# Graph attention edges: four runs per partition with sums of their own, and a stitch of 512 runs

## The reference

```python
feat = (h @ W).reshape(n, H, F)                    # H = 4 heads of F = 64
e = leaky_relu(el[src] + er[dst], 0.2)             # el, er: a score per node and head
m = segment_max(e, dst); ex = exp(e - m[dst])
a = ex / segment_sum(ex, dst)[dst]
out = segment_sum(feat[src] * a[:, :, None], dst)  # then + b, elu
```

## Time and profile before

| | us |
|---|---|
| median of 3 runs | 7038.84 (7034.03 to 7040.12) |
| profiled execution | 7034.15 |
| its span, from first to last instruction | 7032.2 |

### The profile page before, as it was taken

How to read it: one execution, slowest core, us unless ns; L and a number is a source line. 1 busy time by engine, 2 the same in 40 slices (tenths; PEclk the granted TensorE clock), 3 DMA queues, 4 the chain that set the end, 5 groups by cost and what they waited for, 6 DMA issues and landing times. The chain is left out here.

```text
span 7032.2 us, 58077 instructions
## 1 busy us (share of the span) xinstructions
PE 2366.4 (34%) x11337; PEld 1626.9 (23%) x11337; DVE 5315.1 (76%) x9732; ACT 2257.9 (32%) x5114; POOL 5123.8 (73%) x5324
## 2 busy tenths in 40 slices
PE   5899998998995870000000000035000000000000
PEld 4555555555553660000000000023000000000000
DVE  8899999999996786666667666653666666667676
ACT  4788888888885530000000000022000000000002
POOL 5777777777774557777777777767777777777775
PEclk9999999999997995555555555567555555555555
DMA  8677777777775596666666666644566666666667
GB/s 286 195 213 215 212 215 213 214 213 214 213 215 154 143 230 203 213 232 218 220 231 213 233 218 213 235 141 122 192 222 226 213 235 216 228 223 213 235 234 260
DMA packets 680849, 1500.22 MB, mean 213 GB/s; under 512 B 164313, under 2 KB 497566, under 8 KB 667420
## 3 DMA queue, kind: packets, MB, share of 16 engines
q0 software_dynamic: 250192, 691.16, 33.7%
q1 hardware_dynamic: 430540, 807.88, 33.0%
HBM read 772.63 MB, written 727.42 MB: 213 GB/s over the span
## 5 line engine op out<-in xcount | busy, mean ns | idle before, releaser
L1815 POOL DMA_INDIRECT gb_g<-table,ix_g x3126 | 2966.6, 949 | 953.0 <-issue 952.1
L586 POOL DMA_INDIRECT gb<-table,src x1563 | 1518.0, 971 | 483.6 <-issue 476.1
L1915 DVE SCALAR_TENSOR_TENSOR gb_g<-gb_g,same_g,wv 128x256 f32<-128x256 f32 x3024 | 1449.0, 479 | 83.9
L1097 PE MATMUL pm<-ident,tl 128*4 128x128 f32 x2 | 0.7, 372 | 3991.6 <-DMA tl<-sums 3991.6
L1842 ACT ACTIVATE ww<-ee 128x132 f32<-128x132 f32 (+3 forms) x102 | 28.5, 280 | 3609.5 <-DVE ee L1893 3609.5
L620 PE MATMUL po<-parts,sel 128*128 128x256 f32 x3930 | 956.6, 390 | 68.5 <-DVE parts L730 66.8
L1903 DVE TENSOR_TENSOR wv<-gb_g,ww 128x1024 f32<-128x1024 f32 x782 | 954.5, 1221 | 0.0
L1097 PEld LDWEIGHTS pm<-ident,tl 128*4 128x4 f32 x2 | 0.2, 82 | 3992.4 <-DMA tl<-sums 3992.4
L1885 DVE TENSOR_TENSOR ee<-gb_g,held 128x128 f32<-128x128 f32 (+3 forms) x102 | 36.5, 358 | 1077.2 <-DMA gb_g<-table,ix_g 1077.2
L620 PEld LDWEIGHTS po<-parts,sel 128*128 128x128 f32 x3930 | 716.4, 190 | 295.0 <-DVE parts L730 166.5
L667 ACT ACTIVATE sq<-iota_f,behind 128x128 f32<-128x128 f32 x1568 | 502.0, 409 | 0.0
(11 more groups left out here) (304 smaller groups left out, 4288.0 us busy)
## 6 DMA issues: line engine op xcount, KB each, us to landing
sums<-gb_g SPq DMA_DIRECT2D x94, 4352.0 KB, 14.3
sums<-ost SPq DMA_DIRECT2D x393, 512.0 KB, 3.3
gb_g<-table,ix_g POOLq DMA_INDIRECT x3126, 2.8
table<-f SPq DMA_DIRECT2D x48, 544.0 KB, 3.9
gb<-table,src POOLq DMA_INDIRECT x1563, 3.0
x<-in_x SPq DMA_DIRECT2D x50, 256.0 KB, 4.9
at<-in_rbf SPq DMA_DIRECT2D x100, 128.0 KB
hT_d<-hT SPq DMA_DIRECT2D x49, 256.0 KB, 4.3
```

What stands on the lines that cost most here:

```text
L586: eng.indirect_dma_start(out=gb[:, group(k), half(k) + j, 0:4, :].rearrange("p a c -> p (a c)"), out_offset=None, in_=q.table0[:, :], in_o ...
L1815: eng.indirect_dma_start(out=gb[:, p, j, :], out_offset=None, in_=q.table1[:, :], in_offset=bass.IndirectOffsetOnAxis(ap=ix[:, s * SBT + j ...
L1915: ins = eng.scalar_tensor_tensor(rows[:, t0 + t, 0:D], row, same[:, t:t + 1], wv[k % 2][:, j, :], ALU.mult, ALU.add)
```

## The change

Each partition's edges become four runs (`Q`) of 391 (`CQ`), so that there are 512 runs of their own sums. A batch of 32 edges per partition is now 8 (`SQ`) of each run. `weighted(t)` multiplies edge t of all four runs; behind one wait stand the product for the next t and then four sums, which belong to four runs and don't read each other. `acc` has four rows. A partition has 1564 edges instead of 1563, so there is one gather more in each layer, and the parts at the end are 4, 4, 4 and 3 edges of each run (16, 16, 16, 12 gathers). In the score tiles each run has a column of its own for what is carried over (144 columns for 132). The store of a batch goes to four places per partition: 512 blocks of 8704 bytes. The last part is stored edge by edge, in 512 blocks of 1088 bytes. The masks, `samep` (now bf16) and the indices are laid out by run. `chunk_stitch` joins 512 runs: four gathers, four scatters, and rows four times as long in every step between. The 4-partition copy of the links between runs (`chunk_whole`) is made there, no longer in `stitch`.

```diff
+Q = 4
+CQ = -(-E // (Q * P))
+CE = Q * CQ
+SQ = SBT // Q
-ENDS = [(SB - 2, 0, 16), (SB - 2, 16, SBT)] + [(SB - 1, t, min(t + m, LAST)) for t, m in ((0, 15), (15, 17)) if t < LAST]
+ENDS = [(SB - 2, 0, 4), (SB - 2, 4, SQ)] + [(SB - 1, t, min(t + 4, LAST)) for t in (0, 4) if t < LAST]
...
 # stitch
-                        eng.tensor_tensor_scan(lead[:, 1:], q.samep[:, 1:CE], q.samep[:, 1:CE], 1.0, ALU.mult, ALU.mult).then_inc(s_seg, 1)
+                        for k in range(Q):
+                            ins = eng.tensor_tensor_scan(lead[:, k, 1:], q.samep[:, k, 1:CQ], q.samep[:, k, 1:CQ], 1.0, ALU.mult, ALU.mult)
...
 # gat_edges: store, gathers, sums
-                    eng.dma_start(out_v[:, s * SBT:(s + 1) * SBT, :], gb[:, p, :, :]).then_inc(s_st[p].sem, 16)
+                    eng.dma_start(out_v[:, :, s * SQ:(s + 1) * SQ, :], gb[:, p, :, :, :]).then_inc(s_st[p].sem, 16)
...
+                def rows(s, t, p, signal):
+                    for k in range(Q):
+                        eng.indirect_dma_start(out=gb[:, p, k, t, :], out_offset=None, in_=q.table1[:, :],
...
                     for t in range(m):
                         after(k_row)
-                        ins = eng.scalar_tensor_tensor(rows[:, t0 + t, 0:D], row, same[:, t:t + 1], wv[k % 2][:, j, :], ALU.mult, ALU.add)
+                        if t + 1 < m:
+                            ins = weighted(t + 1)
+                        for k in range(Q):
+                            row = acc[:, k, :] if t == 0 else rows[:, k, t0 + t - 1, 0:D]
+                            ins = eng.scalar_tensor_tensor(rows[:, k, t0 + t, 0:D], row, same[:, k, t:t + 1], wv[t % 2][:, k, :], ALU.mult, ALU.add)
...
 # chunk_stitch: POOL
-                eng.indirect_dma_start(out=hd[:, :], out_offset=None, in_=q.sums1_x, in_offset=col(q.chunk_head, 0)).then_inc(s_hd, 16)
-                eng.wait_ge(s_fin, 1)
+                for k in range(Q):
+                    eng.indirect_dma_start(out=hd[:, k, :], out_offset=None, in_=q.sums1_x, in_offset=col(q.chunk_head, k)).then_inc(s_hd, 16)
+                for k in range(Q):
+                    eng.wait_ge(s_fin, k + 1)
+                    eng.indirect_dma_start(out=q.sums1_x, out_offset=col(q.chunk_fix, k), in_=hd[:, k, :], in_offset=None,
...
 # chunk_stitch: DVE
+                eng.wait_ge(s_hd, 16 * Q)
...
+                for k in range(0, Q, 2):
+                    eng.wait_ge(s_out, k // 2 + 1)
```

More of the change, by code:

```diff
@@ L877, in segments @@
+                        eng.tensor_reduce(first[:, :], lead[:, :, :], X, ALU.add).then_inc(s_seg, 1)
                     else:
@@ L1828, in _ @@
                     free(s, s // B, s % B)
-                    for j in range(SBT):
-                        rows(s, j, s % B, s_g[s % B].sem)
+                    for t in range(SQ):
+                        rows(s, t, s % B, s_g[s % B].sem)
                 for x, (s, t0, t1) in enumerate(ENDS):
@@ L1833, in _ @@
                         free(s, s // B, s % B)
-                    for j in range(t0, t1):
-                        rows(s, j, s % B, s_ge[x])
+                    for t in range(t0, t1):
+                        rows(s, t, s % B, s_ge[x])
             @block.scalar
@@ L1880, in body @@
                     eng.sem_clear(s_dv)
-                    eng.tensor_copy(same[:, 0:m], q.samep[:, here])
+                    eng.tensor_copy(same[:, :, 0:m], q.samep[:, :, here])
                     eng.wait_ge(s_seg.sem, s_seg.at(s, back=1))
@@ L1938, in _ @@
-                    eng.tensor_scalar(add[:, :, 1:], bc(flags, 1, [P, H, m]), BIG, -BIG, ALU.mult, ALU.add).then_inc(s_mask, 1)
-                    eng.tensor_scalar(back[:, :, 1:], bc(flags[:, ::-1], 1, [P, H, m]), BIG, -BIG, ALU.mult, ALU.add).then_inc(s_mask, 1)
+                    add, back, mul = (y[:, :].rearrange("p (h k t) -> p h k t", h=H, k=Q) for y in masks)
+                    opened = [y[:, :].rearrange("p (x t) -> p x t", t=m + 1)[:, :, 0:1] for y in masks]
+                    flags = q.samep[:, :, s * SQ + t0:s * SQ + t1]
@@ new lines, in _ @@
+                    for y, v in zip(opened, (-BIG, -BIG, 0.0)):
+                        eng.memset(y, v).then_inc(s_mask, 1)
+                    eng.tensor_copy(mul[:, :, :, 1:], bc(flags, 1, [P, H, Q, m])).then_inc(s_mask, 1)
+                    eng.tensor_scalar(add[:, :, :, 1:], bc(flags, 1, [P, H, Q, m]), BIG, -BIG, ALU.mult, ALU.add).then_inc(s_mask, 1)
+                    eng.tensor_scalar(back[:, :, :, 1:], bc(flags[:, ::-1, ::-1], 1, [P, H, Q, m]), BIG, -BIG, ALU.mult, ALU.add).then_inc(s_mask, 1)
```

320 lines of the change are left out of this document (164 added, 156 removed).

## The result

| | before | after |
|---|---|---|
| median, first comparison (6 runs each) | 7038.76 us | 7061.39 us |
| ratio after / before | | 1.003 [1.002, 1.004] |
| profiled execution | 7034.15 us | 7044.43 us |
| median, second comparison (9 and 5 runs) | 7029.42 us | 7055.55 us |
| ratio | | 1.0035 [1.0021, 1.0049] |

The change costs 0.3 to 0.35%, 23 to 26 us. The two profiled executions are only 10.3 us apart; the first experiment shows in which stages the rest of the difference lies.

A forecast was written before the change was run, and what follows sets the result against it. POOL's gathers were taken to pace the edges, with DVE counting only after the last ones. Terms -6.7 + 0.3 + 1.6 + 31.4 + 0.6 - 0.5 = +26.7 us gave 7065 us, 0.38% slower, range 7050 to 7082.

The forecast's parts named there:

- Gathers pace the edges: In gat_edges POOL's gathers, 1.254 us each and waiting for nobody, set the pace; DVE's savings go into its wait.
- Price of the sums: In gat_edges a step of one product and four sums takes 2.75 us against 3.07; a batch falls from 27.95 to 26.1.
- DVE's chain: DVE's work from the start of batch 46 to the end of gat_edges: 82.5 us, where it was 85.9.
- End of the edges: From batch 46's last gather to the last sum in gat_edges: 89.3 us, so -6.7 in the first layer, +0.3 in the second.
- the lateness of batch 46: Delay from batch 46's last gather being issued to DVE's start on it: 2.2 to 6 us with the smaller store blocks.
- the arrival bound: Last gathers, their landing and the last part's work end gat_edges 89.3 us after batch 46's last gather, in both layers.
- The first rival: In gat_edges stores still delay gathers, batch 46 lands 8 to 12 us late: +6.4 on the forecast, 7072 us; chance 0.15.
- Last stores: After the last sum of gat_edges, two pieces in blocks of 1088 bytes take longer to land: +0.8 us each layer.
- Stitch: chunk_stitch is a chain with nothing beside it, so everything that grows counts: +15.7 us each layer, +31.4 for both.
- The rival "made of latencies": chunk_stitch steps are mostly hops between engines that don't grow with width: +7 us a stitch, 7048 us in all; chance 0.13.
- Layer 0's `stitch`: In layer 0's stitch, lead becomes four scans, a copy and a turn go, bf16 masks may be faster: -0.5 us.
- Index loads: A layer's first indices are 512 pieces of 32 bytes: +0.3 us each, 0 to 1.

The follow-up runs named there:

- the first experiment: Changed kernel rerun unaltered: 7055.55 us against 7029.42; both chunk_stitch stages left out of the changed kernel: 6993.26 us, and of the kernel before: 6997.13 us.
- after_wait_each: Changed kernel with a wait ahead of every sum again, runs, stores and stitch kept: 7070.56 us.
- after_store4: Changed kernel with each batch's store split into two transfers, in blocks of 4352 bytes instead of 8704: 7050.34 us (its before 7029.69).
- before_no_join: Kernel before with both chunk_stitch stages left out, so the output is not the reference's: 6997.13 us.

## Why the prediction was right

The forecast was +26.7 us; the medians say +22.6 and +26.1. Its steps:

- **Gathers pace the edges.** Right: 1.253 us with "issue" ahead, and `after_wait_each` moved 192 us of DVE's work with the time moving by 15.0, about what the ends give.
- **Price of the sums.** 2.75 forecast, 2.82 measured. The product starts 4523.03 - 4521.35 = 1.68 us after the first of the four sums, where 1.62 was forecast: the sums start (1.65 - 0.47) / 3 = 0.39 apart, not 0.37. Batch 46 fell from 27.95 to 26.75 and not to 26.1, and DVE's chain from there on takes 91.4 - 7.2 = 84.2 us and not 82.5. So DVE saved 1.2 us in a batch and not 1.85, and its wait for rows grew by 100 us and not by some 180. The saving exists, though: the rule of the Trainium skill (VectorE: DVE Perf Modes, "The DRAIN you can't avoid"), that semaphores cost nothing extra there, which it gives for copies, doesn't fit 2.82 against 3.08.
- **End of the edges.** -6.7 and +0.3 forecast; -4.6 and +2.5 measured in the profiled pair, and the two ends are equal, as forecast. Two steps failed together, by 2.1 us in each layer. One is the lateness of batch 46, 2.2 to 6 forecast and 7.2 measured. The prediction took the share of 64 packets in the earlier trace rows as spread over the whole store. It is a head start of about 4 us and turns afterwards, and halving the blocks left 6.4. The other is DVE's chain: 7.2 + 82.5 would have been 89.7, only 0.4 above the arrival bound, and the other 1.7 are the chain's 84.2. The forecast had DVE wait for rows in the last parts; it worked without a pause from batch 46 on. The first rival (lateness 8 to 12) had the mechanism nearly right, that DVE's chain sets both ends, and its price of 6.4 us was 4.3. The Trainium skill (DMA: Bandwidth & Descriptors, "Queues, rings and completion order") names 9 to 17 descriptors before an engine changes queues. With a block counted as a descriptor, the first 4 us, 168 / 16 = 10.5 blocks an engine, would fit; the 348 / 16 = 22 of `after_store4` and the turns afterwards don't.
- **Last stores.** +0.8 each: from the last sum to the read of `tl` 4604.50 - 4599.12 = 5.38, where it was 4.55. Right.
- **Stitch.** +15.7 forecast, +16.5 and +16.4 measured, and right step by step in the table above. The largest miss is the scatters: the first one lasts 1.48, so the row of four takes 4.4 and not 3.9. With its 0.30 of issue, that one is over the 1.3 us that the prediction had named as a sign of being wrong; it cost 0.5. The rival "made of latencies" (7 us) is out.
- **Layer 0's `stitch`.** -0.5 forecast, -3.6 measured, beyond its bound of -2: POOL's span there falls from 54.4 to 50.8 (50.3 to 51.4 in the other runs of the change, 54.1 to 55.1 in those of before). DVE comes from `samep` to `lead` in 3.66 us instead of 6.22, which is 2.6 of it; where the rest comes from isn't shown. With flags in bf16, the first two of the three masks cost 0.68 each and no longer 1.78. The first one before, and `samep` with that mask and `lead` after:

```profile
2230.97 1.79 DVE L864 CAST seg_mul<-samep 128x1568 bf16<-128x1568 f32 x1
```
```profile
2225.17 1.78 DVE L866 TENSOR_TENSOR samep<-c 128x1564 bf16<-128x1564 int32 x1
...
2226.99 0.68 DVE L869 COPY seg_mul<-samep 128x1568 bf16<-128x1568 bf16 x1
...
2228.83 3.55 DVE L878 TENSOR_TENSOR_SCAN lead<-samep 128x390 f32<-128x390 bf16 x4
```

- **Index loads.** +0.3 each forecast, +0.5 measured: from the issue of the loads to the first gather it takes 2.5 us in both layers, where it took 1.9.

These pieces sum to -2.1 + 1.7 + 32.9 - 3.6 + 1.1 = +30.0. The touched stages as a whole differ by 26.9 in the first pair, since the gathers up to batch 46 took 1.4 and 1.6 us less in the changed kernel; two profiles with the same edges, before and `before_no_join`, lie 2 us apart there. The medians' 22.6 and 26.1 lie below the sum of the pieces, and the runs don't show where. The errors of the terms, +4.3 (edges), -3.1 (layer 0) and +1.5 (stitch), partly cancelled, so the total is better than its terms: that is luck.

## What to carry to other kernels

An engine that is busy 76% can still be off the path: before making it cheaper, read what its longest wait ends on, and count only the stretch behind the last transfer. Splitting a chain into more independent runs moves the work to where they are joined; if nothing runs beside that join, every step of it counts at full price, and the steps can be priced one by one from the old trace. Where gathers share the DMA engines with large stores, look at when a store starts as well as at how its blocks are cut: here moving it took 5.4 us off the lateness, and halving its blocks 0.8.

## What was not expected of the hardware

- A store of 4352 KB has the DMA engines nearly alone for its first 4 us (168 blocks of 8704 bytes, or 348 of 4352, against 16 and 34 gather packets) and takes turns with the gathers afterwards (289 blocks to 254 packets, or 571 to 282, in the next 8 us). What sets these 4 us wasn't found.
- PE's granted clock stood at 0.50 during 6.3 us in which PE was busy throughout. It had been 0.93 in the 4 us before, in which PE had waited for 1.30 us.
- One untouched stage, `gat_output` of the first pair, took 258 to 270 us from run to run. That spread is about half of what this change costs, and enough to mislead a reader of one profile of each kernel.
